# Three attention layers: first values by 0/1 products inside the logits loop instead of 49 scatters, and 42 staged groups instead of 34

## What is computed

```python
def _gat_conv(x, src, dst, ea, W, a_src, a_dst, We, a_edge, bias):
    n = x.shape[0]
    loops = jnp.arange(n, dtype=src.dtype)
    s = jnp.concatenate([src, loops])
    d = jnp.concatenate([dst, loops])
    ea_full = jnp.concatenate([ea, jnp.broadcast_to(ea.mean(0), (n, ea.shape[1]))], 0)
    h = x @ W
    al_s = h @ a_src
    al_d = h @ a_dst
    al_e = ea_full @ We @ a_edge
    alpha = jax.nn.leaky_relu(al_s[s] + al_d[d] + al_e, 0.2)
    amax = jax.ops.segment_max(alpha, d, num_segments=n)
    ex = jnp.exp(alpha - amax[d])
    denom = jax.ops.segment_sum(ex, d, num_segments=n)
    coef = ex / (denom[d] + 1e-16)
    out = jax.ops.segment_sum(h[s] * coef[:, None], d, num_segments=n)
    return out + bias
```

## Time and profile before

| | us |
|---|---|
| median of three runs (lowest, highest) | 8029.91 (8023.18, 8036.19) |
| profiled execution, its own time | 8054.18 |
| span of the profile | 8052.4 |
| busy TensorE (PE) | 4992.3 (62%) |
| busy VectorE (DVE) | 5109.5 (63%) |
| busy ScalarE (ACT) | 1997.5 (25%) |
| busy GpSimd (POOL) | 4907.7 (61%) |
| mean granted TensorE clock | 0.733 of full |

### The profile page before, as it was taken

One profiled execution on the slowest core, in us unless ns is written; L12 is line 12 of the kernel. 1 busy time (PEld: TensorE's weight loads), 2 busy tenths in 40 slices (PEclk: granted clock), 3 DMA queues, 4 the chain that ended last, 5 costly groups with the idle time before them and its releaser, 6 DMA issues.

```text
span 8052.4 us, 102051 instructions
## 1 busy us (share of the span) xinstructions
PE 4992.3 (62%) x25982; PEld 3297.7 (41%) x25982; DVE 5109.5 (63%) x17152; ACT 1997.5 (25%) x3703; POOL 4907.7 (61%) x5045
## 2 busy tenths in 40 slices
PE   5665556666557776799999773542664533754532
PEld 3444443333334444444444442542434533424532
DVE  7787567777769999700001496853797844787744
ACT  6666654433336666500000000000100000000000
POOL 6777747777657777400000477777677776777774
PEclk8777777777778878899999755755656756557756
DMA  6555557777525655588888433421233321234321
GB/s 178 164 155 156 155 153 200 199 198 200 154 65 208 217 206 208 210 302 292 278 291 290 143 99 110 120 60 36 72 117 106 116 52 43 77 113 124 92 53 32
DMA packets 728902, 1216.88 MB, mean 151 GB/s; under 512 B 109340, under 2 KB 547085, under 8 KB 714832
## 3 DMA queue, kind: packets, MB, share of 16 engines
q1 hardware_dynamic: 552716, 847.76, 31.6%
q0 software_dynamic: 161120, 311.32, 15.3%
q10 hardware_dynamic: 14688, 53.48, 1.7%
HBM read 865.31 MB, written 346.85 MB: 151 GB/s over the span
## 4 chain that ended last, share of the span: by engine, by line
POOL 53%; issue 19%; PE 17%; DVE 8%; DMA 1%; ACT 0%; DVEq 0%; SPq 0%; POOLq 0%; ACTq 0%
POOL RO L974 27%; POOL RO L1015 24%; PE PS L1536 13%; DVE RO L2372 2%; PE PS L1649 2%; POOL nd L997 2%; DVE H L2384 2%; POOL acc L1032 1%; DMA RO<-table,src_t 0%; PE PS L1367 0%; PE PS L1340 0%; PE PS L1494 0%; DVE H L2454 0%; DVE H L2455 0%; PE PS L1375 0%
## 5 line engine op out<-in xcount | busy, mean ns | idle before, releaser
L1015 POOL DMA_INDIRECT RO<-table,src_t x2346 | 2245.1, 957 | 1998.1 <-DMA table<-H 1240.0
L974 POOL DMA_INDIRECT RO<-table,src_t x2346 | 2319.4, 989 | 936.3 <-issue 761.2
L1974 DVE TENSOR_TENSOR acc<-acc,PS 128x128 f32 x3910 | 1104.5, 282 | 1064.0 <-PE PS L1576 752.9
L1576 PE MATMUL PS<-RO 128*128 128x128 f32 x3060 | 685.3, 414 | 1159.1 <-DMA RO<-table,src_t 1130.4
L1576 PEld LDWEIGHTS PS<-RO 128*128 128x128 f32 x3060 | 633.3, 315 | 1204.3 <-DMA RO<-table,src_t 1182.1
L2190 DVE TENSOR_SCALAR RO<-PS,loc_t,shared 128x128 f32<-128x128 f32 x2346 | 953.4, 408 | 0.6
L1494 PE MATMUL PS<-RO 128*128 128x128 f32 x3128 | 605.6, 373 | 393.4 <-DMA RO<-table,src_t 378.7
L1494 PEld LDWEIGHTS PS<-RO 128*128 128x128 f32 x3128 | 571.2, 280 | 486.2 <-DMA RO<-table,src_t 461.4
L1280 ACT ACTIVATE small<-small 128x49 f32<-128x49 f32 x3 | 0.7, 245 | 2020.9 <-DVE small L2436 2020.9
L1140 ACT ACTIVATE H<-PS 128x392 f32<-128x392 f32 x784 | 394.6, 503 | 431.5 <-PE PS L1474 427.8
L1649 PEld LDWEIGHTS PS<-als_bf,RO 128*128 128x128 bf16 x7056 | 308.3, 119 | 426.8 <-DVE RO L2372 269.8
(11 more groups left out here) (399 smaller groups left out, 8601.4 us busy)
## 6 DMA issues: line engine op xcount, KB each, us to landing
GT<-adjacency SPq DMA_DIRECT2D x126, 1792.0 KB, 7.2
adjacency<-H SPq DMA_DIRECT2D x98, 1568.0 KB
RO<-adjacency SPq DMA_DIRECT2D x42, 1792.0 KB, 7.3
RO<-table,src_t POOLq DMA_INDIRECT x4692, 3.2
staged<-RO ACTq DMA_DIRECT2D x102, 512.0 KB
H<-staged SPq DMA_DIRECT2D x102, 512.0 KB
soft_rows<-shared SPq DMA_DIRECT2D x196, 256.0 KB
H<-soft_rows SPq DMA_DIRECT2D x98, 512.0 KB, 3.9
```

The costliest lines, as they stand in the source:

```text
L974: pool.indirect_dma_start(rows[:, h * HT + j, :], None, table[k % 2], at(src_t[:, t:t + 1]))\
L1015: pool.indirect_dma_start(rows[:, g % 2 * HT + j, :], None, table[k % 2], at(src_t[:, t:t + 1]))\
L1576: last = mm(PS[:, o:o + D], block[:, j * D:(j + 1) * D], onehot[:, h * HT + j, :], start=True, stop=True)
L1974: tt(at, at, window_at(k, c, j), ALU.add).then_inc(added[h], 1 if j < n - 1 else HT - n + 1)
```

## The change

- The 49 scatters of each attention layer, the array `at_first`, its clearing and its reload are gone.
- Instead each turn of the logits loop handles one node tile (there are 49 turns and 49 node tiles). `first_hots` on VectorE writes a 128x128 tile that is 1 where a node's first edge lies in partition m of the layout by run, and a 128x784 tile that holds `ald_n` of the node in the column of its first edge. `first_values` on TensorE multiplies the two (448 and 336 columns, float32) and adds all 49 products up in two PSUM banks, which are copied to `Gs[1]` in the last turn.
- The own edge's logit is no longer spread over the edges. The edges' exponentials are taken against the maximum over edges alone; `self_weights` joins the own edge with a second factor, exp(edge maximum - common maximum), in one activation of 98 columns. One linked scan and one maximum fall away, and a copy of 784 columns comes behind the input of the exponential.
- SG goes from 34 to 42: eight more groups are stored and taken back, the exponential stands behind 42 stores, and GpSimd's wait for TensorE begins at group 44.

```diff
-SG = 34
+SG = 42
-SCATTER_AFTER = 8
...
-                    sp.wait_ge(first_sc, 16 * NT * (l + 1))
-                    sp.dma_start(G[:, ET:3 * ET], at_first.rearrange("(p j) c -> p (j c)", p=P)).then_inc(first_ld, 16)
...
-                    if g == SCATTER_AFTER:
-                        scatter_firsts(l)
...
-                    nc.scalar.activation(exs_n, exs_n, ACT.Exp).then_inc(exp_out, 1)
+                    nc.scalar.activation(edge_and_self, edge_and_self, ACT.Exp).then_inc(exp_out, 1)
...
+                def first_values(t):
+
+                    pe.wait_ge(first_hot, t + 1 + l * NT)
+                    for to, part in first_parts:
+                        opening = isinstance(t, int) and t == 0
+                        last = mm(to, first_lane, first_row[:, part], start=opening, stop=True,
+                                  skip_group_check=not opening)
+                    last.then_inc(first_added, 1)
...
+                with pe.Fori(1, ITERS - 1) as i:
                     for h in range(2):
                         candidates(i, h)
+                        if h == 0:
+                            first_values(i)
                         spread(i + 1, h)
...
-                step(copy(nd3[:, :, 0], ald_n))
-                step(copy(nd3[:, :, 1], self_n), first_in)
+                step(copy(place_n, firstpos[:]), first_in)
+                step(ts(lane_n, place_n, 0.5, 1.0 / ET, ALU.add, ALU.mult))
+                step(ts(lane_n, lane_n, -0.5, MAGIC, ALU.add, ALU.add))
+                step(ts(lane_n, lane_n, -MAGIC, None, ALU.add))
+                step(stt(place_n, lane_n, -float(ET), place_n, ALU.mult, ALU.add))
+                for q in range(ET // TB):
+                    step(ts(place_iota[:, q * TB:(q + 1) * TB], iota_row[:, 0:TB], float(q * TB), None, ALU.add))
...
+                def first_hots(t):
+                    v.wait_ge(first_added, t + l * NT)
+                    hold(v)
+                    lane = ts(first_lane, iota_row[:], lane_n[:, ds(t, 1)], None, ALU.is_equal)
+                    if isinstance(t, int):
+                        step(lane)
+                    ts(first_row, place_iota, place_n[:, ds(t, 1)], ald_n[:, ds(t, 1)], ALU.is_equal, ALU.mult)\
+                        .then_inc(first_hot, 1)
...
                 make_lo(0, 0)
+                first_hots(0)
                 with v.Fori(0, ITERS - 1) as i:
                     make_lo(i, 1)
                     pick(i, 0)
                     make_lo(i + 1, 0)
                     pick(i, 1)
+                    first_hots(i + 1)
                 make_lo(ITERS - 1, 1)
                 pick(ITERS - 1, 0)
+                v.wait_ge(first_added, (l + 1) * NT)
+                for of, part in first_parts:
+                    step(copy(Gs[1][:, part], of))
                 pick(ITERS - 1, 1)
...
-                v.wait_ge(first_ld, 16 * (l + 1))
-                step(scan(*linked_scan(Gs[4], same_s[:], at_f[:, :, 1], spread, col(ALLSAME), 0.0)))
...
-                step(tt(at_l[:, :, 1], Gs[7], Gs[4], ALU.max))
-                step(tt(Gs[5], Gs[0], at_l[:, :, 1], ALU.subtract), exp_in)
+                step(tt(Gs[5], Gs[0], Gs[7], ALU.subtract), exp_in)
+                step(copy(at_l[:, :, 1], Gs[7]))
...
-                step(tt(exs_n, self_n, amax_n, ALU.subtract), exp_in)
+                step(tt(exs_n, self_n, amax_n, ALU.subtract))
+                step(tt(edge_share, nd3[:, :, 1], amax_n, ALU.subtract), exp_in)
                 v.wait_ge(exp_out, 2 * (l + 1))
-                step(tt(rden_n, nd3[:, :, 0], exs_n, ALU.add))
+                step(tt(rden_n, nd3[:, :, 0], edge_share, ALU.mult))
+                step(tt(rden_n, rden_n, exs_n, ALU.add))
                 step(ts(rden_n, rden_n, 1e-16, None, ALU.add))
                 step(recip(rden_n, rden_n))
                 step(tt(own_weight_ps, exs_n, rden_n, ALU.mult))
+                step(tt(rden_n, rden_n, edge_share, ALU.mult))
```

More of the change, by code:

```diff
@@ L417, in build @@
         back = H[:, ACCW - 2 * GROUP_WORDS:ACCW]
-        at_f = G[:, ET:3 * ET].rearrange("p (j c) -> p j c", c=2)
+        lane_n, place_n = nd[:, 0:NT], nd[:, NT:2 * NT]
+        first_row = acc[:, 3 * ET:4 * ET]
+        place_iota = acc[:, 4 * ET:5 * ET]
+        first_lane = acc[:, 5 * ET:5 * ET + P]
+        first_parts = [(PS[:, 3072:3072 + 4 * TB], slice(0, 4 * TB)), (PS[:, 3584:3584 + 3 * TB], slice(4 * TB, ET))]
         at_l = H[:, 0:2 * ET].rearrange("p (j c) -> p j c", c=2)
@@ L426, in build @@
         als_n, ald_n, self_n, amax_n, exs_n, rden_n = (small[:, i * NT:(i + 1) * NT] for i in range(6))
+        edge_and_self, edge_share = small[:, 3 * NT:5 * NT], amax_n
         mean_var = small[:, 6 * NT:8 * NT].rearrange("p (t c) -> p t c", c=2)
@@ L594, in build @@
         first_in = sem("first_in")
-        first_sc = sem("first_sc")
-        first_ld = sem("first_ld")
+        first_hot = sem("first_hot")
+        first_added = sem("first_added")
         last_in = sem("last_in")
@@ L912, in _ @@
                     neighbour_edges()
-                    sp.wait_ge(zeros_ready, 1)
-                    sp.dma_start(at_first.rearrange("(p j) c -> p (j c)", p=P), acc[:, 0:2 * ET]).then_inc(zeros_stored, 16)
                     other_inputs()
@@ L984, in in_step_with_logits @@
                         pool.wait_ge(al_rows[1], i - LOGITS_BEHIND + l * ITERS)
[L986 to L991, removed]
                 def gather_lasts(l):
@@ L1655, in attention @@
                     spread(0, h)
-                with pe.Fori(0, ITERS - 1) as i:
+                candidates(0, 0)
+                first_values(0)
+                spread(1, 0)
+                candidates(0, 1)
+                spread(1, 1)
+                with pe.Fori(1, ITERS - 1) as i:
                     for h in range(2):
                         candidates(i, h)
+                        if h == 0:
+                            first_values(i)
                         spread(i + 1, h)
+                candidates(ITERS - 1, 0)
+                first_values(ITERS - 1)
+                candidates(ITERS - 1, 1)
                 for h in range(2):
-                    candidates(ITERS - 1, h)
                     pe.wait_ge(al_done[h], ITERS + l * ITERS)
@@ L1666, in attention @@
                 pe.wait_ge(turn_blk, l + 1)
-                carries(5)
+                carries(4)
                 pe.wait_ge(ex_loaded, 16 * (l + 1))
@@ L1982, in edge_pass @@
                     beside_pass(-1)
-                    v.wait_ge(zeros_stored, 16)
                 for c in range(NG):
@@ L2403, in attention @@
                     step(stt(Gs[5], attr3[:, :, c], col(VV + 3 * l + c), Gs[5], ALU.mult, ALU.add))
-                v.wait_ge(first_ld, 16 * (l + 1))
                 add, spread = (ALU.add, ALU.max), (ALU.mult, ALU.add)
-                step(scan(*linked_scan(Gs[3], same_s[:], at_f[:, :, 0], spread, col(ALLSAME), 0.0)))
-                step(scan(*linked_scan(Gs[4], same_s[:], at_f[:, :, 1], spread, col(ALLSAME), 0.0)))
+                step(scan(*linked_scan(Gs[3], same_s[:], Gs[1], spread, col(ALLSAME), 0.0)))
                 v.wait_ge(al_loaded, 16 * (l + 1))
@@ L2501, in _ @@
                     first_ranks()
-                    step(memset(acc[:], 0.0), zeros_ready)
+                    step(memset(acc[:], 0.0))
                 if k in DENSE:
```

3 lines of the change are left out of this document (removed).

## The result

| | before | after |
|---|---|---|
| median (lowest to highest) of four runs each, us | 8031.5 (8023.2 to 8036.2) | 7963.0 (7960.3 to 7967.8) |
| profiled execution, its own time | 8054.2 | 7964.4 |
| span | 8052.4 | 7962.6 |
| mean granted TensorE clock | 0.733 | 0.742 |

The account below looks back on a forecast made before the run. GpSimd's list of gathers and scatters was taken to bound each attention layer. Scatters removed, 189.3 us, less new waits of 98.3, left 91 us won: 8,029.9 - 91 = 7,939 us, range 7,841 to 8,025.

Parts of the forecast that it names:

- What goes: Attention layers, GpSimd: 49 scatters of 1.287 us vanish, 63.1 us a layer, 189.3 in all if GpSimd never waits.
- The gate: Before the exponential on ScalarE: it waits for staged group 41, so 431.4 us after the layer's first gather instead of 414.5.
- The loop: Logits loop: a turn grows from 5.36 to 7.45 us, +2.1 us 48 times, +101 us a layer.
- GpSimd's own pace: GpSimd's gathers up to group 44: without scatters due 452.9 us into layer one, 454.1 in the other two.
- The waits: GpSimd at group 44 waits for the weighted pass's first product: 19.5, 39.4 and 39.4 us, 98.3 in all.
- Behind group 44: GpSimd from group 44 to the last gather: 609.9 us in layer one, 610.7 in the others, left unchanged.
- rival D: Little or no gain, or step pairs in the alternating stretch passing 10 us: 7,990 to 8,040 us; chance 0.12.
- The clock: TensorE in the logits loop: granted clock 0.50 to 0.6, so the new product takes 2.65 us at 1.2 GHz.
- Rival C: Logits loop: the dense product lifts TensorE's clock, 6.7 us a turn, nearly all 189 us won, 7,841 to 7,870; chance 0.20.
- The median: Whole kernel: profiled execution lies 24.3 us above the median, so 91 us comes off 8,029.9, giving 7,939.
- a circle of 7.5 us: Logits loop, TensorE and VectorE: product, spread, comparison, picks and operands wait on each other in a closed round of 7.5 us.
- an engine list of 6.3: Logits loop, VectorE: its own work with the two new operands, 0.9 us more a turn, makes 6.3 us.

Follow-up runs that it names:

- the run with the first tile alone: Changed kernel with operands and product made for the first node tile only, 48 of 49 tiles of first values left out; 7850.4 us, ratio 0.9757.
- the one of 6.23: Changed kernel with the new product cut to 56 + 56 columns in all turns but the first, VectorE's operands kept; 7840.4 us, ratio 0.9749.

## Why the prediction was right

The mechanism, the place and the sign were right; the gain was 68 us instead of 91. The time lies well inside the range of 7,841 to 8,025, but that range spans almost everything from the whole gain to none; what the prediction earned is seen in its terms. By the traces:

- **What goes.** 63.1 us a layer: confirmed by the run with the first tile alone, whose layers are 62.5 to 64.1 us shorter than before.
- **The gate.** The exponential has left it, as forecast, and VectorE releases it.
- **The loop.** This term was mis-sized, though its mechanism was right. A turn was put at 7.45 us (sum of links 2.95 + 0.92 + 1.20 + 1.49 + 0.91); it is 7.71, 7.77 and 7.71 in the mean of each layer. Medians over the turns: product 3.03 from the operands' end (0.08 more), from there to the comparison 1.11 (0.19 more: the prediction let the spread overlap the product's end by 0.1 us and the comparison start with the spread's end, while the rows show 0.07 and then 0.15 more), comparison 1.20, the picks 1.5 to 1.6, operands 0.88. The loop so took 113 to 116 us a layer more than before instead of 103. The exponential came 459.1, 483.0 and 478.7 us into the layer, forecast as 450.4 and twice 471.5.
- **GpSimd's own pace.** Group 44 was due at 452.9 and twice at 454.1; GpSimd reached it at 460.4, 456.7 and 460.4. The gathers' delays in the loop were priced at 5 us a layer and came to 9.2 to 11.7: of 147 operations 103 delayed a gather by over 0.05 us, 0.7 of them where 0.4 had been assumed. They fall inside the wait, as said, so they cost nothing here.
- **The waits.** 21.1, 48.6 and 40.6 us (the rows above less 0.30 of issue), forecast 19.5, 39.4 and 39.4. Layers 1,089, 1,114 and 1,107, forecast 1,083 and twice 1,105: 19.5 us in all, which is the miss by the traces.
- **Behind group 44.** 607.8, 608.6 and 606.3 us, taken as 609.9 and 610.7. Nothing waits there, and rival D did not come; it does come with 48 staged groups, by a path that the prediction did not have (the last rows, not a pair of steps over 10 us).
- **The clock.** 0.55 to 0.60 in the loop, as forecast; all but two of 147 products took 3 us, as priced at 1.2 GHz. Rival C did not come in this order.
- **A misreading without effect.** The loop does not begin 12 us later after the first gather in layers two and three: in the trace of before its first comparison comes 47.6, 68.0 and 67.5 us after that gather, so about 20 us later. The sum goes by the measured 380.0 and is not touched.
- **The median.** The sum was made from a profiled execution 24 us above its median, and 19 us of that lay upstream; taking the difference off the median was right.

The weakest part of the prediction is what it did not draw from its own figures: it wrote down a circle of 7.5 us beside an engine list of 6.3, and did not say that another order of the same instructions would be worth most of the difference. Nor did it add up TensorE's own list, from its rows 2.65 + 2 x 1.18 + 2 x 1.03 = 7.07 us, which is what bounds the turn once the circle is cut.

## What to carry to other kernels

When two engines hand work to each other in a loop, add up every closed circle of waits as well as each engine's list. Here the longest set the turn in each order that was run, and an operation on an engine idle a sixth of the time cost nearly its full length. Put a product whose result nobody in the loop reads where it delays nothing that the other engine is waiting for, as late in the turn as its buffer allows. A buffer of staged work buys time for a late producer, but look where its end meets the next phase: here 46 groups fit and 48 did not.

## What the runs showed of the hardware

Gathers and VectorE's 0.68 us operation from SBUF do hold each other up, both ways, depending on who starts when. The changed kernel, layer one, one pair of each kind:

```profile
4749.79 0.68 DVE L2390 TENSOR_SCALAR acc<-acc,nd,small 128x784 f32<-128x784 f32 x1
...
4750.00 1.29 POOL L1002 DMA_INDIRECT RO<-table,src_t  x1 [0.30 <-issue]
...
4834.01 0.94 POOL L1002 DMA_INDIRECT RO<-table,src_t  x1 [0.30 <-issue]
...
4834.50 0.85 DVE L2390 TENSOR_SCALAR acc<-acc,nd,small 128x784 f32<-128x784 f32 x1
```

A gather that starts 0.2 us into the operation takes about 1.29 us instead of 0.94 (82 cases in the three layers); an operation that starts 0.5 us into a gather takes about 0.85 instead of 0.68 (22 cases). One that starts earlier in a gather is not held up: in the run with the operation twice, 113 of the 114 that started 0.4 us into a gather took 0.68 or 0.69 us. The Trainium skill (SBUF — State Buffer, "SBUF: two separate sides") has the port pair as a lock in both directions, and the prediction denied the half of it in which VectorE waits; the trace agrees with the page that either can be held up. It does not show a lock for the whole of a gather: the operation lost 0.17 us where 0.44 of the gather's 0.94 were still to come, and nothing where 0.54 were. Here the measurement decides.

Who is hit, and how often, depends on how the two engines meet. At 7.7 us a turn 103 of 147 operations delayed a gather; at 6.23 us, close to five issue periods of 1.25 us, 124 of 147 operations started 0.6 us behind a gather's start, and only 8 delayed one. The two engines fall into step. The gathers' delay is therefore no constant of the operation: it was 9 to 12 us a layer in one loop, 2 to 3 in the one of 6.8 us and about 1 in the one of 6.23, with the same instructions on VectorE. It did not vanish there, but passed in part to VectorE: those 124 operations took 0.77 us instead of 0.68, some 4 us a layer, on the engine whose list is the turn.

Not tried: the own edges' new form by itself, which lies behind the waits measured here, and a kernel that keeps TensorE's clock at its higher level through the loop.
